# A two-layer compressed interaction network with table gathers: products from four arrays of features instead of five, two fill banks, quarter blocks, W1 sent for early

## What is computed

```python
e = jnp.stack([tbl_0[ids[:, 0]], ..., tbl_38[ids[:, 38]]], axis=1)
for W in [W0, W1]:                               # (39*39, 128), (39*128, 128)
    z = jnp.einsum('bmd,bnd->bdmn', X0, Xi)      # X0 = e; Xi = e, then layer 1's output
    Xi = jnp.einsum('bdp,po->bod', z.reshape(z.shape[0], z.shape[1], M0 * mi), W)
    res.append(Xi)
h = jnp.concatenate([jnp.sum(jnp.concatenate(res, axis=1), axis=-1), dense_ctx], axis=1)
h = jnp.maximum(h @ W_top1 + b_top1, 0.0)
h = jnp.maximum(h @ W_top2 + b_top2, 0.0)
y = h @ W_top3
```

## Time and profile before

| | us |
|---|---|
| median of 3 runs | 230.61 (230.29 to 232.42) |
| the profiled execution, its own time | 230.19 |
| its span in the profile | 228.6 |

### The profile page before, as it was taken

One profiled execution on the slowest core, in us unless ns is written; L12 is line 12 of the kernel. 1 busy time (PEld: TensorE's weight loads), 2 busy tenths in 40 slices (PEclk: granted clock), 3 DMA queues, 4 the chain that ended last, 5 costly groups with the idle time before them and its releaser, 6 DMA issues.

```text
span 228.6 us, 4760 instructions
## 1 busy us (share of the span) xinstructions
PE 204.9 (90%) x1715; PEld 156.0 (68%) x1715; DVE 176.5 (77%) x295; ACT 167.6 (73%) x300; POOL 109.2 (48%) x106
## 2 busy tenths in 40 slices
PE   4577956879989998999999899799999999999995
PEld 4577813435556566777787577577778888889794
DVE  0899956999869899999979998798899787532010
ACT  6999465769867999798879998697867575775003
POOL 4788777777777777877777778000000000000000
PEclk9999779999999999999999999999999999999999
DMA  5950000240392591200240000003100000000000
GB/s 143 217 128 7 9 7 6 65 69 6 77 236 66 70 314 29 44 5 7 65 65 7 7 7 7 1 3 94 22 3 0 0 3 0 1 0 3 0 0 3
DMA packets 22015, 10.26 MB, mean 45 GB/s; under 512 B 11576, under 2 KB 20877, under 8 KB 21992
## 3 DMA queue, kind: packets, MB, share of 16 engines
q1 hardware_dynamic: 18728, 9.11, 16.4%
q0 software_dynamic: 3264, 0.84, 3.9%
HBM read 8.63 MB, written 1.31 MB: 44 GB/s over the span
## 4 chain that ended last, share of the span: by engine, by line
PE 60%; DVE 17%; ACT 9%; issue 7%; DMA 4%; POOL 1%; SPq 1%; DVEq 0%; ACTq 0%
PE s_bank L1013 14%; PE side_bank L967 6%; PE side_bank L969 6%; PE side_bank L968 6%; PE g_bank L995 4%; DVE z L786 3%; DVE z_lo L796 3%; DVE w_sb L725 3%; PE b_bank L947 3%; PE side_bank L962 3%; PE side_bank L995 3%; PE side_bank L934 3%; PE side_bank L975 2%; DMA feat<-tbl,ids_sb 2%; PE side_bank L912 2%
## 5 line engine op out<-in xcount | busy, mean ns | idle before, releaser
L387 POOL DMA_INDIRECT feat<-tbl,ids_sb x102 | 109.0, 1069 | 33.3 <-issue 21.9
L575 ACT ACTIVATE z_hi<-z 128x512 fp32r<-128x512 f32 x100 | 61.9, 632 | 10.6 <-DVE z L786 8.7
L786 DVE TENSOR_TENSOR z<-factors,b_bank 128x512 f32<-128x512 f32 x84 | 57.1, 681 | 7.9 <-PE b_bank L947 3.7
L796 DVE TENSOR_TENSOR z_lo<-z,z_hi 128x512 fp32r<-128x512 f32 x84 | 57.8, 688 | 0.3 <-ACT z_hi L575 0.2
L1013 PE MATMUL s_bank<-g,w_sb 128*128 128x128 f32 x312 | 47.5, 279 | 0.0
L1013 PEld LDWEIGHTS s_bank<-g,w_sb 128*128 128x128 f32 x312 | 44.1, 192 | 4.8 <-issue 2.4
L967 PE MATMUL side_bank<-z_hi,w_hi 128*128 128x512 f32 x84 | 42.3, 504 | 0.0
L969 PE MATMUL side_bank<-z_hi,w_lo 128*128 128x512 f32 x84 | 33.2, 396 | 0.0
L968 PE MATMUL side_bank<-z_lo,w_hi 128*128 128x512 f32 x84 | 32.9, 392 | 0.0
L467 ACT ACTIVATE factors<-side_bank 128x512 f32<-128x512 f32 x31 | 18.4, 594 | 7.2 <-PE side_bank L934 7.2
L947 PE MATMUL b_bank<-xs,sel 117*128 117x512 bf16 x48 | 18.7, 389 | 1.4 <-DVE direct_z L786 0.8
(11 more groups left out here) (181 smaller groups left out, 333.0 us busy)
## 6 DMA issues: line engine op xcount, KB each, us to landing
w_sb<-w SPq DMA_DIRECT2D x3, 832.0 KB, 5.8
feat<-tbl,ids_sb POOLq DMA_INDIRECT x102, 2.4
lines<-line SPq DMA_DIRECT2D x4, 320.0 KB, 2.2
diag<-lines SPq DMA_DIRECT2D x32, 40.0 KB
wt_sb<-wt SPq DMA_DIRECT2D x2, 512.0 KB
g<-small SPq DMA_DIRECT2D x1, 770.0 KB
g<-small SPq DMA_DIRECT2D x1, 448.0 KB
w0p<-w_pair SPq DMA_DIRECT2D x1, 448.0 KB
```

Source lines behind the costliest of these rows:

```text
L387: nc.gpsimd.indirect_dma_start(feat[:, bt % 2, n * D:(n + 1) * D], None, tables[order[n]], bass.IndirectOffsetOnAxis(ids_sb[:, bt, n:n + 1 ...
L575: nc.scalar.activation(z_hi[:, s % RING, :], z[:, at, :], ACT.Copy).then_inc(rounded, 1)
L786: nc.vector.tensor_tensor(target, one, other, ALU.mult).then_inc(product, 1)
L796: nc.vector.tensor_sub(low[rows, s % RING, :], z[rows, SPLITS[s] % Z_RING, :], z_hi[rows, s % RING, :].bitcast(f32)).then_inc(remainder, 1)
```

## The change

- Rows of four features, all six pairs of them used: three arrays "a", "b", "c" are copied to SBUF (`COPIES`), one stays in PSUM (`b_bank[0]`). `ORDER` says which two a step multiplies: steps 0, 1, 2 and 6 take both from SBUF, steps 3, 4 and 5 one from PSUM. `_factors` assigns pairs to rows anew (tables `FOURS`, `THREES`); the weights of layer 1 follow on the host. A chunk has 4 selection matmuls for 5, and 3 copies on ACT for 2. `F_RING` is 2 for 3.
- Two fill banks: "b" and the first turn of x go to `turn_bank`, "a", "c" and the second turn of x to the freed `b_bank[1]`.
- Quarter blocks: `BANDS` is 4, so `g_block` has 16 matmuls of 32 rows by 80 columns for 8 of 64 by 160, the banks at the side first, and signals once when all are done. Waits on `g_copied` are for one copy less (`- 1`), since the first copy frees the side banks. `diag` and its zeros are half as large.
- W1 is sent for, all three pieces, when tile 0's features have been turned, ahead of the first `spread_lines`; the dense layers' weights at chunk 1 for 5.
- `PACED_FROM` is 40 for 33: gather n waits until n - 39 steps of layer 1 are done.

The functions around them in `after.py` (whose lines are other ones: multiply L790, rest_z L800, select L946, fill L938, g_block L994) are the same. The core of the diff:

```diff
--- before.py
+++ after.py
@@ -33,10 +33,16 @@
 PT = 7
 REST_T = PT - 1
 REST_LO = slice(64, 64 + F)
-SELECTS = 3
-BASES = ((0, 5, 10, 13, 20), (0, 14, 3, 16, 21), (0, 8, 12, 14, 17))
-CHAIN = (1, 3, 0, 2, 4)
-LEAD = 2
+COPIES = "abc"
+ARRAYS = len(COPIES) + 1
+ORDER = ((0, 1), (0, 2), (1, 2), (0, 3), (1, 3), (2, 3), (0, 0))
+SELECT_AT = 1
+TURNS, LEVELS = 9, 4
+FOURS = (((0, 1), (1, 1), (3, 2), (8, 2)), ((0, 0), (1, 2), (2, 2), (7, 3)), ((0, 0), (5, 2), (6, 3), (7, 2)),
...
+         ((0, 0), (0, 1), (0, 2), (0, 3)))
+THREES = (((0, 1), (4, 2), (7, 3)), ((0, 0), (3, 2), (1, 3)), ((0, 0), (2, 1), (2, 3)))
 CH = 512
 CB = CH // D
 CPT = P // CB
@@ -47,12 +53,11 @@
 STEPS = CHUNKS * PT
 SPT = CPT * PT
 LAG = 5
-B_RING = 2
 DIRECT = [[1, 3, 5], [], [], []]
 WHOLE = 3
 Z_LAG = 2
 Z_RING = 6
-F_RING = 3
+F_RING = 2
 RING = LAG + 2
 assert RING == PT
 LOOK_P = 125
@@ -66,29 +71,26 @@
 FREE_FIRST = 8
 WARM = (3, 8, 2)
 BETWEEN, BETWEEN_FROM = 2, 13
-PACED_FROM = 33
-W1_AT = [3, 3, 4]
-W1_PIECES = len(W1_AT)
-MLP_IN = 5
+PACED_FROM = 40
+W1_PIECES = 3
+MLP_IN = 1
 COPY_XI = PT - 1 + LAG
 TURN_XI = COPY_XI + 2
 G_AT = TURN_XI + 2
-BANDS = 2
+BANDS = 4
 HB = SB // BANDS
 SETS = 4 // BANDS
 SET_SUBS = SUBS // SETS
 G_COLS = SET_SUBS * HB * GW
 GPC = 2
-FILL_A = 4
-FILL_B = 3
+FILL_AT = (2, 3, 5)
 EMBED_AT = [12, SPT + 2]
 SPLIT_AT = [[], [8, 14, 19], [7, 14, 21], [7, 14, 21]]
 LINE_AT = [[1, 2, 3, 4], [13, 16, 21], [12, 19, 26], [12, 19, 26]]
 X_AT = [[], [21, 23], [23, 24], [23, 24]]
-A_AT = [0, 24, 25, 25]
-B_AT = [0, 25, 26, 26]
+NEXT_FILL_AT = [(), (25, 26, 26), (25, 26, 26), (25, 26, 26)]
 S2_AT = SPT - PT + G_AT + 3
 S2_STEPS = [SPT - 2] * (TILES - 2) + [16]
 TOP_AT = [64, 92, 113, 115, 116]
@@ -258,14 +260,14 @@
-        b_bank = [bank(f"b_bank{j}") for j in range(B_RING)]
+        b_bank = [bank(f"b_bank{j}") for j in range(2)]
-        turn_banks = [turn_bank, g_banks[1], l1_bank[1], b_bank[1][:]]
+        turn_banks = [turn_bank, b_bank[1][:], g_banks[1], l1_bank[0], l1_bank[1]]
@@ -331,25 +333,31 @@
+        def factors_due(s):
+            bt, v = divmod(s, SPT)
+            due = []
+            for name, at, next_at in zip(COPIES, FILL_AT, NEXT_FILL_AT[(bt + 1) % TILES] or [None] * len(COPIES)):
+                if (i := chunk_at(s, at)) is not None and (i + 1) % CPT:
+                    due.append((name, i + 1))
+                if bt + 1 < TILES and v == next_at:
+                    due.append((name, CPT * (bt + 1)))
+            return due
+        fills = [[("x", 0, 0)], [("a", 0, 0)], [("x", 0, 1)], [("b", 0, 0)], [("c", 0, 0)]]
+        bank_of = {"a": 1, "b": 0, "c": 1}
+                        fills[k].append(("x", bt + 1, k))
+            for name, i in factors_due(s):
+                fills[bank_of[name]].append((name, i, 0))
...
@@ -423,6 +431,10 @@
+            sp.wait_ge(*after(turn_filled, "x", 0, XJ - 1))
+            for k in range(W1_PIECES):
+                m = slice(k * F // W1_PIECES, (k + 1) * F // W1_PIECES)
+                sp.dma_start(w1_sb[:, m, :], w1.rearrange("(m n) o -> n m o", n=O)[:, m, :]).then_inc(w1_in, 16)
@@ -433,10 +445,6 @@
-                for k, at in enumerate(W1_AT):
-                    if i == at:
-                        m = slice(k * F // W1_PIECES, (k + 1) * F // W1_PIECES)
-                        sp.dma_start(w1_sb[:, m, :], w1.rearrange("(m n) o -> n m o", n=O)[:, m, :]).then_inc(w1_in, 16)
@@ -579,8 +588,8 @@
-                for half, pair in enumerate((g_bank[:, :, :], side_bank[:, i % 2:i % 2 + 2, :])):
-                    act.wait_ge(g_summed, SETS * i + half + 1)
+                for half, pair in enumerate((side_bank[:, i % 2:i % 2 + 2, :], g_bank[:, :, :])):
+                    act.wait_ge(g_summed, SETS * i + min(half + 1, SETS))
@@ -774,15 +781,12 @@
-                k, j = u % 2, u // 2
-                if u < 2:
-                    dve.wait_ge(*after(turn_taken, "ab"[u], i, 0))
-                one = factors[:, i % F_RING, k, :]
-                if u == REST_T:
-                    other = one
-                else:
-                    dve.wait_ge(selected, SELECTS * i + j + 1)
-                    other = b_bank[(SELECTS * i + j) % B_RING][:]
+                for k, name in enumerate(COPIES):
+                    if u == max(k - 1, 0):
+                        dve.wait_ge(*after(turn_taken, name, i, 0))
+                if u == len(COPIES):
+                    dve.wait_ge(selected, i + 1)
+                one, other = (factors[:, i % F_RING, k, :] if k < len(COPIES) else b_bank[0][:] for k in ORDER[u])
@@ -899,7 +903,7 @@
-                    pe.wait_ge(g_copied, GPC * g_before_fill[n])
+                    pe.wait_ge(g_copied, GPC * g_before_fill[n] - 1)
@@ -931,20 +935,15 @@
-                nc.tensor.matmul(turn_banks[k], sel[:, SELECTS + "ab".index(name), :], columns(i // CPT, i % CPT),
+                nc.tensor.matmul(turn_banks[k], sel[:, COPIES.index(name), :], columns(i // CPT, i % CPT),
-            def select(i, j):
-                q = SELECTS * i + j
-                if j == 0:
-                    features_there(i)
-                if q >= B_RING:
-                    before, number = divmod(q - B_RING, SELECTS)
-                    pe.wait_ge(product, PT * before + 2 * number + 2)
-                elif q == 1:
-                    pe.wait_ge(*after(turn_taken, "b", 0, 0))
-                nc.tensor.matmul(b_bank[q % B_RING][:], sel[:, j, :], columns(*divmod(i, CPT)),
+            def select(i):
+                features_there(i)
+                if i:
+                    pe.wait_ge(product, PT * (i - 1) + REST_T)
+                nc.tensor.matmul(b_bank[0][:], sel[:, ARRAYS - 1, :], columns(*divmod(i, CPT)),
@@ -957,7 +956,7 @@
-                    pe.wait_ge(g_copied, GPC * (i - 1))
+                    pe.wait_ge(g_copied, GPC * (i - 1) - 1)
@@ -990,7 +989,7 @@
-                        to = [*g_banks, *side][BANDS * (r // SET_SUBS) + h]
+                        to = [*side, *g_banks][BANDS * (r // SET_SUBS) + h]
```

More of the change, by code:

```diff
@@ L658, in _ @@
                     take_xit(i)
[L659 to L662 removed]
+                for name, i in factors_due(s):
+                    if i % CPT:
+                        take_factor(name, i)
                 if 1 <= bt < TILES - 1:
@@ L817, in _ @@
                 if s == 0:
[L818 removed]
+                    take_x(CB, P, turn_taken[fill["x", 0, 1][0]])
                 if s == CTX_CHUNK * PT:
@@ L1182, in _factors, with point @@
 def _factors():
-    rows = [None] * P
-    base_at = [list(range(F)), [*range(F, REST_LO.start), *range(REST_LO.stop, P)], list(range(REST_LO.start, REST_LO.stop))]
-    second = np.zeros(P, bool)
-    for k, base in enumerate(BASES):
-        for n, p in zip(range(F), base_at[k]):
-            rows[p] = [(n + x) % F for x in base]
-            second[p] = k == 1
-    for n, p in zip(range(0, F, 4), base_at[1][F:]):
-        rows[p] = [(n + x) % F for x in CHAIN]
-    factors = np.full((SELECTS + 2, P), -1)
+    def point(i, level):
+        return TURNS * level + i % TURNS
@@ new lines, in _factors @@
+    fixed = [TURNS * LEVELS + k for k in range(F - TURNS * LEVELS)]
+    blocks = [tuple(point(i + n, level) for i, level in block) for block in FOURS for n in range(TURNS)]
+    for k, block in enumerate(THREES):
+        blocks += [(fixed[k], *(point(i + n, level) for i, level in block)) for n in range(TURNS)]
+        blocks += [(fixed[k], *(point(n + step, k) for step in range(0, TURNS, TURNS // 3))) for n in range(TURNS // 3)]
+    blocks.append(tuple(fixed))
+    base_at = [list(range(F)), [*range(F, REST_LO.start), *range(REST_LO.stop, P)][:F], list(range(REST_LO.start, REST_LO.stop))]
@@ new lines, in _factors, with lead @@
+    others = [p for p in range(P) if not any(p in at for at in base_at)]
+    holder = {}
+    def lead(n, tried):
+        for x in blocks[n]:
+            for k in range(len(base_at)):
+                if (x, k) not in tried:
+                    tried.add((x, k))
+                    if (x, k) not in holder or lead(holder[x, k], tried):
+                        holder[x, k] = n
+                        return True
+        return False
+    for n in range(len(blocks)):
+        lead(n, set())
@@ L1199, in _factors @@
+    assert len(holder) == len(base_at) * F
+    rows = {base_at[k][x]: (x, *(y for y in blocks[n] if y != x)) for (x, k), n in holder.items()}
+    rows.update(zip(others, [block for n, block in enumerate(blocks) if n not in holder.values()]))
+    assert len(rows) == len(blocks) <= P
+    second = np.zeros(P, bool)
+    second[base_at[1]] = True
+    factors = np.full((ARRAYS, P), -1)
     pairs = np.full((PT, P, 2), -1)
     seen = set()
-    for p in range(P):
-        if rows[p] is None:
-            continue
-        factors[SELECTS:, p], factors[0:SELECTS, p] = rows[p][0:2], rows[p][2:]
+    for p, row in rows.items():
+        factors[0:len(row), p] = row
@@ L1205, in _factors @@
         for t in range(REST_T):
```

(13 more changed lines are left out.)

61 lines of the change are left out of this document (22 added, 39 removed), and 2 rows, old and new, of the table FOURS.

## The result

The changed kernel takes 238.72 us (median of 6 executions, 234.25 to 245.40) against 230.58 us of the kernel before, timed beside it. The ratio is 1.022, 95% interval 1.018 to 1.027; it is taken from the three shorter executions (234.25, 235.40 and 235.69 us), because the other three (241.75 to 245.40 us) fell into a slower state of the chip. Timed again, the kernel took 238.59 us (4 executions), a ratio of 1.035 (1.028 to 1.042). The change makes the kernel slower by 2 to 4%. The prediction was slower, 235.8 us; the time lies inside its range. The first profile is of the execution of 241.75 us, so the mechanism is read there and again in a second profile, of 238.93 us.

What follows compares the result with a forecast made beforehand. POOL's gathers until the last lands, then TensorE, were taken to bound the kernel. Span 228.6 + 5.6 - 0.9 + 1.1 - 0.6 = 233.8, plus 1.6 around it and 0.42 for the median: 235.8 us; four-in-five range 224.5 to 252.

Steps and rivals of the forecast that it cites:

- POOL as a second clock: POOL's unbroken 102 gathers set the pace beside the engines; time gained before the last one lands (144.2 us) is waited off.
- the wait for VectorE as the cause: Gathers begun inside a VectorE instruction with both inputs in SBUF wait it out, and the next of that kind; 8.5 us lost.
- Products from SBUF, +5.6 us: Products 0, 1 and 2 with both inputs in SBUF make the last gather land 5.6 us later: +3.2 and +2.4.
- the prediction's signs: Among them: last gather starts near 147 us, not 141.8; the 78 gathers busy near 87 us; a block about 1.5 us.
- I take it in all seven: Gathers at all seven squares of tiles 1 and 2 lose 1.06 us, instead of four of them: +3.2 us.
- a second instruction, .60 more: Of eight other gathers losing 0.15 to 0.41 us, half wait for a second VectorE instruction, 0.60 us more each: +2.4.
- The rival of the whole run: Gathers wait until the whole run of two-SBUF-input instructions is over: 246.7 us, with no break 263; chance 0.15.
- Selections and waits, -.9 and -.6: Last four chunks have one selection less each, -0.9 us; the turn of x needs one copy of `g` only, -0.6.
- quarter blocks, +1.1: Each block on TensorE takes 1.47 us instead of 1.28; six follow the last gather: +1.1 us, ends -3.8 and +7.7.
- The per-instruction price from the look-ups, .046 us: Look-ups, 8 short matmuls in 0.37 us, priced each of a quarter block's 32 instructions: 1.47 us a block.
- Copies and W1 first at 0: 16 more ACT copies hidden by slack and the later gather; W1 sent first delays the first block 5 us at worst: 0.
- the pace at 0: The pacing of gathers held nothing before, and 40 holds less than 33: 0 at both ends.

Runs made afterwards that it cites:

- the alternating kernel: Changed kernel with the same seven products reordered, steps 1, 3 and 5 reading PSUM between those from SBUF: 230.58 us, ratio 1.000; timed again 229.62 us, ratio .993.

## Why the prediction was right, and where it was not

*POOL as a second clock, and the wait for VectorE as the cause: right.* The profile alone gave this, and the kernel before with three more products from SBUF shows it with one edit: 9.9 us later at the gather, 9.9 us longer. What stands behind the last gather does not depend on when it comes: 82.7 to 82.8 us in the second profile, in that with as many products from PSUM as before and in both of the alternating kernel, with last gathers that end between 144.3 and 154.6.

*Products from SBUF, +5.6 us: the term that was mis-sized.* It measured +9.9 alone (kernel before with that edit) and +11.8 to +13.0 in the changed kernel (last gather's end at 154.6 and 155.7 against 142.8). Of the prediction's signs, neither the last gather near 147 nor busy gathers near 87 us came: they were 151.4 and 154.8, and 93.4 and 94.9. Two steps of it failed. "I take it in all seven", at 1.06 us, a price for two instructions: the long waits were six, fewer than seven, but lost 1.16 to 3.29 us each, together 12.5 instead of 7.4 (first profile). A gather pays for as many instructions as stand in the run behind its start, up to six, and not for two. And "a second instruction, .60 more" for half of the short ones, 2.4: the short ones grew by 4.6. The rival of the whole run named the right price for a long wait, as the gather of 4.23 us shows, and "no run of over three exists today" was the reason that I gave against it: an absence in the trace, not evidence. Its sum of 246.7 was too high because most gathers do not pay. A small misreading besides: of the four gathers the one at 130.46 took 1.86 us and lost .92, not 1.06.

*Selections and waits, -.9 and -.6; quarter blocks, +1.1.* From the last gather's end to the end the kernel before has 85.8 us (228.6 - 142.76), the changed one 82.7 in the second profile; the prediction's terms give -.4, measured are -3.1. With the block as measured, -1.3 in place of +1.1, the terms make -2.8. By the alternating kernel without them, 83.8, quarter blocks account for 1.0 of the 3.1, and what is left, 2.1, compares with the 1.5 of selections and waits. The per-instruction price from the look-ups, .046 us, did not carry over: the 32 instructions go out in fours at .11, that is .028 each. But in the kernel before quarter blocks bring nothing behind the last gather (86.1 against 85.8), so what they are worth depends on the rest, and why is open. The rule of the Trainium skill (TensorEngine Tiling (Array Packing), "Theoretical Speedup"), up to 4 times for 32 rows and 2 for 64, would be a block of .64, an estimate: the trace does not agree, it measured 1.06.

*Copies and W1 first at 0; the pace at 0.* The gathers' gap stays at .30 us up to the last: the pace never held one. W1's pieces took longer to landing than in the earlier trace rows:

```profile
w_sb<-w SPq DMA_DIRECT2D x3, 832.0 KB, 8.0
```

The first block came 1.1 us later than in the earlier trace rows (55.2 us; 56.3 in the second profile), under the 5 allowed; no run shows that it reaches the end. Copies: VectorE's wait for factors is 4.8 us in the changed kernel's page; that late gathers hide it is argued, not shown by itself. In the two kernels with five products from PSUM fills and copies come out as the next wait, which fits a cover that was real.

*The total came near by luck, two errors of opposite sign*: the gathers' term was too small by 4 to 7 us in the profiled executions, the block's too large by 2.4. The three executions near 235 us, which hit the forecast best, were not profiled; with 82.7 us behind their last gather (an estimate from the second profile) it ended 7 to 9 us later than before, not 5.6 (spans of 232.6 to 234.1 us). What carried the sign was the place of the last gather. The changed kernel with its products interleaved is within 1% of the kernel before; the only one more than 1% below it computes other pairs.

## What to carry to other kernels

When an engine off TensorE feeds the rest (here POOL's gathers, with a full queue from start to end), every change to the order of VectorE's instructions is a change to that feeder: look at which instructions take both inputs from SBUF and how long they stand in a row, not only at how many there are. Interleaving the same instructions with ones that read PSUM gave back all the 8 us without one operation less. And a chain that a late transfer covers can hide other waits: with the gathers quickened further, by five products from PSUM, TensorE's waits for its fills took the gain.

## What the runs showed of the hardware

A gather that waits beyond one instruction lasts until .90 us after the last of VectorE's two-SBUF-input instructions in a row (its start plus .60), for two to six of them still to come: 2.00, 3.20, 3.30, 4.01 and 4.23 us. The Trainium skill (SBUF — State Buffer, "Who interferes with whom") has the later of the two wait for the earlier; the trace shows up to six instructions waited for, and so goes further than the one.

The instruction in which it starts need not have two inputs: a gather of 3.39 us in the second profile began in a copy from SBUF to SBUF and waited out the four products and remainders behind it.

But whether it waits so long depends on where in the instruction it starts. The count is over the POOL and VectorE timelines of all 14 profiles, from 37.4 us on, of the gathers that began in such an instruction with at least one more behind it (an instruction is reckoned from its start to the next one's, less .02 us). Of 125 that began within .02 us of its start, 103 lost nothing and 21 waited out the run; of 54 from .03 to .12 us, 19 waited out the run, 5 lost nothing and 30 lost .45 to .55 us (one .79), about the one instruction; of 133 later ones, 4 waited out the run, the others lost .44 us at most, the rest of that instruction. An example of the last kind in the changed kernel, begun .37 us into an instruction with two more behind it (POOL, then VectorE):

```profile
86.34 1.26 POOL L395 DMA_INDIRECT feat<-tbl,ids_sb  x1 [0.30 <-issue]
```

```profile
85.97 0.81 DVE L714 TENSOR_TENSOR parts<-rest 128x352 bf16<-128x352 f32 x1
86.69 0.69 DVE L790 TENSOR_TENSOR z<-factors 128x512 f32<-128x512 f32 x1
87.29 0.68 DVE L800 TENSOR_TENSOR z_lo<-z,z_hi 128x512 fp32r<-128x512 f32 x1
```

It is done at 87.60; had it waited out the run, which ends at 87.89, it would have been done at 88.79. For these the rule of the one instruction holds. What decides in the first tenth of a microsecond is open. It is why a loss is a draw per gather, and why one profile of such a kernel should not be taken for all.

TensorE's granted clock fell in the changed kernel behind a stretch in which TensorE had stood waiting. Two-microsecond windows of its first profile, then a row of its waits from 100 to 118 us:

```profile
110.00:112.00 2.00, 0.00 (x0) 0.00 (x0) 1.66 (x4) 1.21 (x3) 1.39 (x3) 0.99 0.03 4
112.00:114.00 2.00, 1.16 (x9) 1.19 (x10) 2.00 (x4) 1.90 (x5) 1.70 (x2) 0.50 0.14 8
114.00:116.00 2.00, 2.00 (x10) 1.60 (x10) 2.00 (x5) 1.50 (x2) 1.39 (x3) 0.50 0.05 4
116.00:118.00 2.00, 2.00 (x12) 1.90 (x11) 1.71 (x3) 1.38 (x2) 1.70 (x2) 0.50 0.10 8
118.00:120.00 2.00, 2.00 (x11) 1.64 (x11) 0.69 (x1) 0.81 (x3) 1.48 (x2) 0.80 0.04 4
```

```profile
PE side_bank L916 <- ACT g L594: 3.7, 1, 3.7
```

It waited 3.7 us, in the end for a copy of `g` that ScalarE makes behind its part of the late features, and then went on at 1.2 GHz (.50 of 2.4) for six microseconds. The second profile has the same twice: granted clocks of .64 and .50 from 98 to 102 us behind a wait of 1.9 us, and of .56 and .59 from 112 to 116 behind one of 3.4. Behind the last gather the two differ: in the first profile, after a wait of 3.7 us, the turn of x takes 1.05 us for the eight matmuls that took .64 before; in the second, after one of 2.4 us, .63 at a clock of 1.00. So a late gather can cost more than its lateness, but need not. How much of the first profile's time is due to each is not split here.
